# Feed-forward scales and x's product on GpSimd, another order of the feed-forward tiles and of one mask load

## What is computed

```python
x = x + attention(layernorm(x), ctx, ctx, bias, mask)   # 16 heads of 16, softmax over 512 keys
x = x + ffn(layernorm(x))

def fp4_quant_dequant(x):                  # blocks of 16 along the last dimension
    scale = max(max(abs(xb)) / 6.0, 1e-12)
    xn = xb / scale
    q = GRID[searchsorted(MID, abs(xn))] * sign(xn) * scale   # GRID 0 .5 1 1.5 2 3 4 6

def fp4_linear(x, w):
    return einsum("bsk,nk->bsn", fp4_quant_dequant(x), fp4_quant_dequant(w))

gate, y = fp4_linear(x, w_gate), fp4_linear(x, w_up)      # 256 -> 704
h = silu(gate) * y
out = fp4_linear(h, w_down)                               # 704 -> 256
```

## Time and profile before

| | |
|---|---|
| median of 3 runs | 955.62 us (954.97 to 956.7) |
| the profiled execution | 958.21 us, of which the span shown is 956.4 |
| busy, share of the span | PE 94%, PEld 74%, DVE 75%, ACT 64%, POOL 56% |
| attention with the weights' quantization | 0 to some 673 us |
| feed-forward | some 673 us to the end |
| loop, 700 to 900 us | PE busy 191 us of 200, DVE 175, ACT 102, POOL 48 |

### The profile page before, as it was taken

The page is one execution under the profiler, slowest core; times in us unless marked ns, Lnnn a source line. Parts: engine busy times, 40 slices in busy tenths (PEclk is TensorE's granted clock), DMA queues, the critical chain, the costliest instruction groups (busy, mean ns, idle before and its releaser), DMA issues.

```text
span 956.4 us, 20203 instructions
## 1 busy us (share of the span) xinstructions
PE 901.2 (94%) x6740; PEld 710.6 (74%) x6740; DVE 713.9 (75%) x1848; ACT 613.9 (64%) x1116; POOL 534.2 (56%) x500
## 2 busy tenths in 40 slices
PE   5798999999999999999999999999889999999997
PEld 4676777777877877777777777676568888888886
DVE  5766667666766767767676598997488888888894
ACT  3466777777776767777767688787645555555542
POOL 5775866776685786777668558765022222222222
PEclk9899999999999999999999999999999999999999
DMA  6586334343343433444234344400000000000000
GB/s 195 162 223 176 105 67 126 106 102 89 90 126 87 112 101 70 122 109 105 81 98 123 90 109 115 117 10 1 2 0 17 17 17 16 16 16 16 16 16 28
DMA packets 50792, 76.45 MB, mean 80 GB/s; under 512 B 5264, under 2 KB 22032, under 8 KB 50704
## 3 DMA queue, kind: packets, MB, share of 16 engines
q1 hardware_dynamic: 50448, 75.06, 29.4%
q10 hardware_dynamic: 256, 0.26, 0.1%
HBM read 45.16 MB, written 29.36 MB: 78 GB/s over the span
## 4 chain that ended last, share of the span: by engine, by line
PE 73%; issue 11%; ACT 5%; DMA 4%; DVE 4%; SPq 3%; POOL 1%; ACTq 0%; DVEq 0%; POOLq 0%
PE psum L1197 24%; PE psum L1334 12%; PE psum L1288 11%; PE psum L1219 4%; PE psum L1528 4%; PE psum L1545 4%; PE psum L1530 3%; PE psum L1529 3%; PE psum L1252 3%; PE psum L1229 2%; DVE att L1130 2%; DMA mask_u<-in_mask_BxS_bk_dram 1%; ACT att L766 1%; ACT att L881 1%; SPq L393 1%
## 5 line engine op out<-in xcount | busy, mean ns | idle before, releaser
L1059 DVE CUSTOM_DVE_ANT_0 att<-psum,att 128x512 f32<-128x512 f32 x512 | 343.5, 686 | 172.6 <-PE psum L1288 171.5
L610 POOL TENSOR_TENSOR att<-att,neg_max 128x512 f32<-128x512 f32 x308 | 322.9, 1059 | 184.1 <-DVE neg_max L1059 181.4
L1197 PE MATMUL psum<-ident,att 128*128 128x128 f32 x2576 | 381.2, 276 | 27.0 <-ACT att L766 15.7
L1197 PEld LDWEIGHTS psum<-ident,att 128*128 128x128 f32 x2576 | 309.1, 141 | 99.1 <-ACT att L766 33.2
L766 ACT ACTIVATE att<-psum 128x512 f32<-128x512 f32 x512 | 299.3, 599 | 126.5 <-PE psum L1197 122.1
L1288 PE MATMUL psum<-stack 128*128 128x512 f32 x512 | 270.8, 530 | 8.7 <-DMA stack<-q_hl 6.8
L691 POOL TENSOR_TENSOR att<-att 128x704 f32<-128x704 f32 x32 | 61.5, 1922 | 180.7 <-DVE att L1175 180.7
L773 ACT ACTIVATE att<-att,neg_max 128x512 f32<-128x512 f32 x204 | 147.0, 721 | 10.1 <-DVE neg_max L1059 10.1
L1288 PEld LDWEIGHTS psum<-stack 128*128 128x128 f32 x512 | 98.2, 192 | 43.4 <-issue 32.7
L1334 PE MATMUL psum<-att 128*32 128x256 f32 x2048 | 124.7, 384 | 0.0
L1545 PE MATMUL psum<-att 128*128 128x256 f32 x384 | 91.7, 380 | 2.7 <-ACT att L889 2.7
(11 more groups left out here) (98 smaller groups left out, 1015.3 us busy)
## 6 DMA issues: line engine op xcount, KB each, us to landing
stack<-qk_planes SPq DMA_DIRECT2D x124, 192.0 KB, 4.0
qk_planes<-k_hl SPq DMA_DIRECT2D x48, 256.0 KB
qk_planes<-q_hl SPq DMA_DIRECT2D x48, 256.0 KB
att<-in_fside_1xSxS_dram SPq DMA_DIRECT2D x32, 256.0 KB, 2.8
att<-in_ctx_dram SPq DMA_DIRECT2D x8, 512.0 KB, 6.6
out_dram<-att SPq DMA_DIRECT2D x32, 128.0 KB, 1.7
x<-in_x_dram SPq DMA_DIRECT2D x1, 2560.0 KB, 14.2
x<-in_x_dram SPq DMA_DIRECT2D x3, 512.0 KB, 7.5
```

Source lines behind the costliest of these rows:

```text
L610: pool.tensor_tensor(prob[:, slot, :], prob[:, slot, :], neg_max[:, slot:slot + 1].to_broadcast([P, S]), ALU.subtract).then_inc(less_pool, 1)
L1059: dve.tensor_tensor_reduce(out=prob[:, slot, :], in0=ps_score[:, SCORE_BANK[2 * S_ + r], :], in1=bias_m[:, tt, :], scale=-1.0, scalar=BIG, ...
L1197: return pe.transpose(out_, in_, ident[:, :])
```

## The change

SyncE issues the next batch's mask load ahead of the load of the rest of x. In the feed-forward steps the block maxima lie in SBUF (f_am) in place of PSUM, and both scales are made by GpSimd from them; GpSimd also makes x's product, ahead of the scales in its step, and h's product after them. It now runs steps -2 to 1 before the last batch's second layernorm scale (rstd2_of). ScalarE takes x_abs(n+2) before silu. VectorE's step has the order L1130, L1125, L1136, L1133, L1145, L1150, L1166, L1162, L1171, L1175, L1179, in lines of the kernel before; L1141, L1159 and L1160 are gone.

```diff
 (SyncE, body)
+                if not last:
+                    wait(sp, maskneg_ready, b + 1)
+                    sp.dma_start(mask_u8[:, :], mask[one(b + 1), :].to_broadcast([P, S])).then_inc(mask_in, 16)
                 if is_first(b):
                     sp.dma_start(x1[:, 3 * NT:ROWS, :], x_v[:, 3 * NT:ROWS, :]).then_inc(xrest_in, 16)
                 if not last:
-                    wait(sp, maskneg_ready, b + 1)
-                    sp.dma_start(mask_u8[:, :], mask[one(b + 1), :].to_broadcast([P, S])).then_inc(mask_in, 16)
...
 (GpSimd, step)
-            rstd2_of(B - 1)
+                if live(mt):
+                    pool.wait_ge(fxd_ready, mt + 1)
+                    wait(pool, fxT_ready, mt - 1)
+                    pool.tensor_tensor(blocks(f_xq[:, 1 - par, :]), blocks(f_xt), spread(f_s[:, 1 - par, NHB:NHB + NXB], NXB),
+                                       ALU.mult).then_inc(fxq_ready, 1)
+                if lo < hi:
+                    if live(mx):
+                        pool.wait_ge(fxm_ready, mx + 1)
+                        wait(pool, fxy_ready, mx)
+                        wait(pool, fxq_ready, mx - 1)
+                    if live(mh):
+                        pool.wait_ge(fhm_ready, mh + 1)
+                        wait(pool, fhy_ready, mh)
+                        wait(pool, fhq_ready, mh - 1)
+                    pool.sem_inc(waited_pool, 1)
+                    pool.tensor_scalar(f_s[:, par, lo:hi], f_am[:, lo:hi], -1.0 / 6.0, -MIN_SCALE, ALU.mult, ALU.min)
+                    pool.tensor_scalar(f_r[:, lo:hi], f_am[:, lo:hi], TIE_DOWN / 6.0, MIN_SCALE, ALU.mult, ALU.max).then_inc(fsr_ready, 1)
...
+            for n in range(-2, 2):
+                step(n, n % 2)
+            rstd2_of(B - 1)
+            ffn_loop(pool, step, 2)
...
 (ScalarE, ffn_step)
+                if live(n + 2):
+                    x_abs(n + 2, par)
                 m = n
                 if live(m):
                     act.wait_ge(fgate_ready, m + 1)
...
                 if live(n + 1):
                     x_parts(n + 1, 1 - par)
-                if live(n + 2):
-                    x_abs(n + 2, par)
...
 (VectorE, step)
-                if live(mt):
-                    dve.wait_ge(fxa_ready, mt + 1)
-                    dve.scalar_tensor_tensor(f_xt, f_xa, MAGIC, f_xy[:, 1 - par, :], ALU.max, ALU.add).then_inc(fxu_ready, 1)
                 if live(mh):
...
                 if live(mt):
+                    dve.wait_ge(fxa_ready, mt + 1)
+                    wait(dve, fxq_ready, mt)
+                    dve.scalar_tensor_tensor(f_xt, f_xa, MAGIC, f_xy[:, 1 - par, :], ALU.max, ALU.add).then_inc(fxu_ready, 1)
+                if live(mx):
+                    dve.wait_ge(fxn_ready, mx + 1)
+                    dve.tensor_reduce(f_am[:, NHB:NHB + NXB], blocks(f_xn[:, par, :]), op=ALU.max, axis=AX.X,
+                                      apply_absolute_value=True).then_inc(fxm_ready, 1)
+                if live(mt):
                     dve.wait_ge(fxu_ready, mt + 1)
                     dve.scalar_tensor_tensor(f_xt, f_xa, MAGIC, f_xt, ALU.max, ALU.subtract).then_inc(fxd_ready, 1)
...
                 if live(m2):
                     dve.wait_ge(fha_ready, m2 + 1)
                     wait(dve, fhq_ready, m2)
                     dve.scalar_tensor_tensor(f_hu, f_ha, MAGIC, f_hy[:, par, :], ALU.max, ALU.add).then_inc(fhu_ready, 1)
+                if lo < hi:
+                    dve.wait_ge(fsr_ready, n + 3)
+                    dve.reciprocal(f_r[:, lo:hi], f_r[:, lo:hi]).then_inc(fr_ready, 1)
```

More of the change, by code:

```diff
@@ L198, in xattn_ffn @@
         f_xq = cut(2, E)
+        f_am = cut(NHB + NXB)
         f_s = cut(2, NHB + NXB)
@@ L223, in xattn_ffn @@
         ps_x, ps_h = psum[:, 3, :], psum[:, 4:6, :].rearrange("p b n -> p (b n)")
-        ps_y, ps_am = psum[:, 6, :].rearrange("p (i n) -> p i n", i=2), psum[:, 7, 0:NHB + NXB]
+        ps_y = psum[:, 6, :].rearrange("p (i n) -> p i n", i=2)
         x0_in, xnext_in, xrest_in, x2_in, w_in_sem, w_out_sem, ctx_in, mask_in, small_in = (
@@ L228, in xattn_ffn @@
         bias_in = [sem(f"bias_in{t}") for t in range(NT)]
-        waited = sem("waited")
+        waited, waited_pool = sem("waited"), sem("waited_pool")
         const_step, ident_ready = sem("const_step"), sem("ident_ready")
@@ L678, in _ @@
             batches(pool, body)
-            rstd2_of(B - 1)
             def step(n, par):
+                mx, mt, mh = n + 2, n + 1, n - 1
+                lo = 0 if live(mh) else NHB
+                hi = NHB + NXB if live(mx) else NHB
+                if live(mt):
[15 more added lines that the diff above has]
+                    pool.tensor_scalar(f_r[:, lo:hi], f_am[:, lo:hi], TIE_DOWN / 6.0, MIN_SCALE, ALU.mult, ALU.max).then_inc(fsr_ready, 1)
                 m = n - 2
@@ L692, in step @@
                                    ALU.mult).then_inc(fhq_ready, 1)
-            ffn_loop(pool, step)
+            for n in range(-2, 2):
+                step(n, n % 2)
+            rstd2_of(B - 1)
+            ffn_loop(pool, step, 2)
         @block.scalar
@@ L1131, in step @@
                 if live(mt):
+                    dve.wait_ge(fxa_ready, mt + 1)
[6 more added lines that the diff above has]
+                if live(mt):
                     dve.wait_ge(fxu_ready, mt + 1)
                     dve.scalar_tensor_tensor(f_xt, f_xa, MAGIC, f_xt, ALU.max, ALU.subtract).then_inc(fxd_ready, 1)
[L1134 to L1142, removed]
                 if live(mh):
                     dve.wait_ge(fh_ready, mh + 1)
-                    dve.tensor_reduce(ps_am[:, 0:NHB], blocks(f_h), op=ALU.max, axis=AX.X, apply_absolute_value=True).then_inc(fhm_ready, 1)
+                    dve.tensor_reduce(f_am[:, 0:NHB], blocks(f_h), op=ALU.max, axis=AX.X, apply_absolute_value=True).then_inc(fhm_ready, 1)
                 if live(mo):
@@ L1151, in step @@
                                       ALU.add).then_inc(fout_ready, 1)
[L1152 to L1162, removed]
                 if live(m2):
```

## The result

The changed kernel takes 969.2 us (median; 968.2 to 970.1) against 955.6: ratio 1.0139, 95% interval 1.0126 to 1.0153, 1.4% slower. The forecast was 960.3, slower, with a range of 948 to 967. The sign was right; the size was not: 13.6 us were lost where 4.7 were forecast, 8.9 more, and the range was missed by 2.2.

The account below looks back on a forecast made before the run. Feed-forward steps of 8.00 us, TensorE's own 7.37 plus waits, and a first-batch mask stall bound the kernel. Mask -4.3, first tiles +2.2, steps +7.0, last tiles -0.2: +4.7 on 955.6 gives 960.3 us, range 948 to 967.

Parts of the forecast that it names:

- Parts 2 and 3: Feed-forward steps: VectorE's queue relieved but a loop closed through ScalarE; GpSimd's scales lengthen it to 8.26 us, 7.0 us lost.
- h: Feed-forward step: time from c, the start of VectorE's maximum of x, to the reciprocal's start; forecast 3.28 us.
- Part 3: GpSimd's scales in feed-forward steps: first held by VectorE's rounding step L1166, giving a period of 8.26 us, 0.26 longer.
- the Sum: Whole kernel: +4.7 us gives 962.9 in the profiled execution; the median taken 2.6 lower, so 960.3.
- Part 4: First feed-forward tiles: hand-overs unhidden and silu's table load after x_abs; +2.2 us at tile 3, bounds 0 and +3.5.
- What bounds the kernel now: Feed-forward steps of 8.00 us against TensorE's own 7.37, lengthened by waits; also a mask-load stall in the first attention batch.
- The closed loop, 4.98 + h: Feed-forward step: the period is 4.98 us from reciprocal round to maximum of x, plus h, if above 7.37.
- Rival C: Feed-forward steps: GpSimd's scales take longer or the first comes later; h = 3.6, 969 us; chance 0.11.
- Rivals A and B: GpSimd's scales: A, first scale precedes L1166, 949.3 to 956.3, chance 0.22; B, engines don't hinder each other, 943.3, chance 0.12.
- The mask load: First attention batch: moving it ahead of the load of x removes the stall; 4.3 us gained, 3.3 to 5.0.
- rival D: First attention batch: the mask move gives nothing, another transfer or engine being late next; 964.6 us; chance 0.05.
- The forecast's own range: Whole kernel: 957.5 to 963.5 us for the forecast proper, which had chance 0.50.

Follow-up runs that it names:

- the last kernel: Changed kernel with both scales back on VectorE, ScalarE's order undone and both rounding steps of h moved forward in VectorE's queue: 936.4 us, ratio 0.9800.
- the second trace of before: The kernel before, unchanged, profiled once more: 955.1 us, span 953.3.

## Why the prediction was right and wrong

The mechanism of Parts 2 and 3 stood: a loop through ScalarE, VectorE and GpSimd, and a first scale held by a rounding step. What failed are three terms of the sum, each of which put the loss too low: h in Part 3 (3.28, measured 3.46; with it the steps lose 12.0 us and not 7.0), the step in the Sum from the trace to the median (2.9 us), and Part 4, the first tiles (2.2, measured 4.1), where a fall of TensorE's clock stood at nothing. In turn:

**What bounds the kernel now:** right. TensorE's own 7.4 us stood in every kernel, and the last reached it.

**The closed loop, 4.98 + h:** right. In after the part from the reciprocal round to the maximum of x is 8.43 - 3.46 = 4.97; in the run with the first rounding step moved 7.80 - 2.84 = 4.96. Both waits at its ends were named beforehand. TensorE's wait for L1130 (0.30 us a step in before) is gone, as forecast, and nothing came of it, since the loop through ScalarE was the longer one. The room beside the loop was smaller than forecast: VectorE waits 0.84 before the maximum of x, not 1.3. That cost nothing.

**h, 3.28:** the mechanism right, the size short by 0.18 (3.46). Three prices, all a little low: the rounding step L1174 runs 0.88 behind the output sum, and not the 0.83 that it takes behind the reciprocal (L1166 in before, and the same instruction in the run with the scales on VectorE), why is not shown (+0.05); the held scale ends 0.28 after it, not 0.22 (+0.06); the second takes 0.42, not 0.35 (+0.07). I had carried over prices of 32 elements with 0.03 for 28 more. Each is small, but there are 27 steps: 4.6 us, with 0.4 more for tile 3, whose matmuls ran partly at 1.2 GHz (granted clock 0.82 over that step, 1.00 in before). Rival C had the size, 969, and a part of the reason (the scales take longer over 60 elements). That it met the median to 0.2 us is luck: its h was 3.6, 8.58 us a step where 8.43 was measured, 4 us too much, and the other terms, which it shared with the forecast, were about as much too little.

**Rivals A and B:** fell. The first scale starts at c+1.90 (804.08 - 802.18), behind L1174's c+1.79, as the forecast put it; and the engines do hinder each other, by 0.63 us a step.

**The first tiles:** +2.2 forecast, about +4.1 measured. Tile 0: +1.1, as forecast (1.2). From tile 0 to 1 the cost is 13.45 - 9.78 = 3.7, where 2.1 was forecast. The 2.1 came as it was laid out: ScalarE waits for VectorE's x times reciprocal, and only then loads the table and makes silu:

```profile
683.72 0.42 ACT L904 ACTIVATE att<-att 128x256 f32<-128x256 f32 x1 [3.77 <-DVE att L1182]
684.15 1.28 ACT L919 ACT_TABLE_LOAD   x1
685.45 0.76 ACT L919 ACTIVATE att<-psum 128x704 f32<-128x704 f32 x1
```

TensorE waits for what ScalarE makes behind silu, and starts the last matmuls of attention (L1263, L1252 in before) 8.50 us after tile 0's first matmul, where it was 6.41: +2.1. The other 1.6 is the clock, to which the forecast gave nothing. The same sixteen matmuls take 5.30 us behind that wait in after, at a granted clock of 0.69, and 3.72 at 1.00 in before:

```profile
686.53 0.38 PE L1566 MATMUL psum<-q_hl,neg_ident 128*128 128x256 f32 x1 [2.71 <-ACT q_hl L894]
...
688.04 5.30 PE L1263 MATMUL psum<-att 128*128 128x256 f32 x16 [0.69 <-ACT att L757]
```

```profile
690.05 3.72 PE L1252 MATMUL psum<-att 128*128 128x256 f32 x16 [0.83 <-ACT att L734]
```

With the scales on VectorE TensorE waits 1.53 there, the matmuls take 3.72, and tile 1 comes 10.70 after tile 0.

Of the two steps after it the first gives back 1.65 and the second takes 1.05: 15.6 us from tile 1 to 3 against 16.2 before, so 0.6 is given back, where I had counted on 1.1.

**The mask load:** the mechanism right (the wait is gone, nothing given back), and 4.3 us was near the 5.0 of the trace (5.2 with 0.2 that after had gained before the stall). But the stall itself differs from execution to execution, and the one profiled had a long one, with a fall of the clock behind it. In the medians the move is worth 2.7, so rival D, a move that gives nothing, fell.

**From the trace to the median:** this is the step with the second largest miss. I took 2.6 us off the profiled sum since the profiled execution of before was that much above its median. By the second trace of before nearly all of that surplus was the mask's stall (2.7 of the 3.1 us between the two spans; the rest, 0.5, had come before it). The change removes this stall, so the surplus must not be taken off the changed kernel too. The traces differ by 10.6 us, the medians by 13.5. The misses together: steps 5.0, first tiles 1.9, mask -0.9, last tiles -0.2, conversion 2.9, in all 8.7 of the 8.9.

**The forecast's own range:** its terms (mask 3.3 to 5.0, first tiles 0 to 3.5) add up to 957.4 to 962.6, and not to 963.5. The result lies outside either.

What stays open: why the mask's load takes longer in some executions, and why TensorE's clock fell behind one of its two stalls and not behind the other. Neither was tried.

## What to carry to other kernels

Lay out the loop that an order of queues closes, link by link, before counting the work taken off an engine: here VectorE lost 0.7 us of work a step and the step grew by 0.43, because the new orders closed a loop, and the removed work came back inside it as hand-overs and a held instruction. Give GpSimd what starts beside single-input work of VectorE and is not awaited at once (x's product: 12 us gained); do not give it two tiny instructions on which VectorE waits while its own two-input instruction runs (the scales, with the reciprocal behind that instruction: 23 us lost). When a change delays TensorE once, work out what the matmuls behind the wait would take at the lower clock too: it may fall (1.6 us at tile 1) or not (behind the shorter mask stall). And when a profiled execution lies above the median, find out where before subtracting the difference.

## What the runs showed of the hardware

- Two engines that hold each other up: a GpSimd tensor_scalar of 0.42 us took 1.05 beside a VectorE instruction with two SBUF inputs that had started 0.11 earlier, and ended 0.28 after it; VectorE's instruction kept its 0.88. In the last kernel x's product on GpSimd, 0.62 us elsewhere, took 1.20 behind such an instruction, at no cost to TensorE.
- An instruction of VectorE with one SBUF input was held too, a float32 tensor_scalar from SBUF to SBUF. In the last kernel it came while GpSimd's product of h ran, to 803.50, and took 0.83; it takes 0.18 in the runs with the scales on VectorE, where GpSimd is idle by then:

```profile
802.11 1.39 POOL L699 TENSOR_TENSOR att<-att 128x704 f32<-128x704 f32 x1
...
802.71 0.83 DVE L1173 TENSOR_SCALAR att<-att 128x60 f32<-128x60 f32 x1
```

  The reduces, of one SBUF input too, were not held: in that kernel the maximum of h keeps its 0.88 beside GpSimd's products; and the weights' reciprocal in the trace of before takes 0.35 beside GpSimd and alone. In the kernel before, with the maxima in PSUM, GpSimd was idle at the tensor_scalar, so nothing could meet there. In the rule of the Trainium skill cited above (same section) this is the other case, an instruction of VectorE in a 2-port performance mode; the traces do not show which mode it ran in.
- A hand-over from VectorE to GpSimd with two more waits and a semaphore step behind the awaited one in the queue took 0.36 us; one from VectorE to ScalarE 0.04.
- One stall of TensorE in two executions of the same kernel, 3.65 us and 2.59 us long, was followed by a fall of the granted clock in the first and by none in the second (0.84 and 1.00 over the next 11 us).
